# A split-precision GRU graph kernel: the products of gates r and z with the aggregate, reordered into high part first and low part last

## What is computed

```
A = (adj != 0).astype(x.dtype)
h = x
for l in range(weight.shape[0]):            # 5 layers
    m = jnp.einsum('bnd,de->bne', h, weight[l])
    agg = jnp.einsum('bij,bid->bjd', A, m)
    h = _gru_cell(agg, h, w_ih, w_hh, b_ih, b_hh)

def _gru_cell(m, h, w_ih, w_hh, b_ih, b_hh):
    gi = m @ w_ih.T + b_ih
    gh = h @ w_hh.T + b_hh
    i_r, i_z, i_n = jnp.split(gi, 3, axis=-1)
    h_r, h_z, h_n = jnp.split(gh, 3, axis=-1)
    r = sigmoid(i_r + h_r)
    z = sigmoid(i_z + h_z)
    n = tanh(i_n + r * h_n)
    return (1.0 - z) * n + z * h
```

## Time and profile before

| | before |
|---|---|
| median of 3 runs | 631.34 us |
| the profiled execution's own time | 631.32 us |
| its span, first to last instruction | 629.2 us |
| mean granted TensorE clock | 0.994 |
| PE busy | 611.5 us, 97% of the span, 2933 matmuls |
| DVE busy | 509.3 us, 81% |
| ACT busy | 411.7 us, 65% |
| POOL busy | 366.6 us, 58% |

### The profile page before, as it was taken

One profiled execution on the slowest core, in us unless ns is written; L12 is line 12 of the kernel. 1 busy time (PEld: TensorE's weight loads), 2 busy tenths in 40 slices (PEclk: granted clock), 3 DMA queues, 4 the chain that ended last, 5 costly groups with the idle time before them and its releaser, 6 DMA issues.

```text
span 629.2 us, 10158 instructions
## 1 busy us (share of the span) xinstructions
PE 611.5 (97%) x2933; PEld 499.0 (79%) x2933; DVE 509.3 (81%) x1163; ACT 411.7 (65%) x777; POOL 366.6 (58%) x299
## 2 busy tenths in 40 slices
PE   7899999999999999999999999999999999999993
PEld 5677888888888888888888888888888888888772
DVE  5987878897878889788897979889797887967677
ACT  4866776758567685766758576675866758564551
POOL 0644645658566565765658576565756657564343
PEclk9999999999999999999999999999999999999997
DMA  7532312220231313022230322223023230000001
GB/s 269 210 101 68 101 67 84 84 101 17 83 100 67 100 47 121 32 83 86 80 100 17 103 81 67 100 83 100 17 83 100 67 100 0 17 0 1 18 0 51
DMA packets 37999, 47.28 MB, mean 75 GB/s; under 512 B 1760, under 2 KB 19680, under 8 KB 37984
## 3 DMA queue, kind: packets, MB, share of 16 engines
q1 hardware_dynamic: 37712, 46.97, 22.7%
q10 hardware_dynamic: 272, 0.13, 0.1%
HBM read 42.90 MB, written 4.19 MB: 75 GB/s over the span
## 4 chain that ended last, share of the span: by engine, by line
PE 92%; DVE 4%; DMA 1%; issue 1%; SPq 1%; ACT 1%; POOL 0%; POOLq 0%; DVEq 0%
PE ps_tok L1244 12%; PE ps_tok L1251 12%; PE ps_r L1109 6%; PE ps_r L1111 6%; PE ps_r L1110 6%; PE ps_z L1111 6%; PE ps_z L1109 6%; PE ps_z L1110 6%; PE ps_tok L1104 5%; PE ps_b L1109 3%; PE ps_b L1111 3%; PE ps_b L1110 3%; PE ps_b L1104 3%; PE ps_in L1110 3%; PE ps_hn L1111 3%; PE ps_in L1109 3%
## 5 line engine op out<-in xcount | busy, mean ns | idle before, releaser
L557 POOL TENSOR_TENSOR h_lo<-h,h_hi 128x512 fp32r<-128x512 f32 x64 | 83.0, 1297 | 113.8 <-ACT h_hi L587 113.8
L567 POOL TENSOR_TENSOR z_h<-z_gate,h 128x512 f32<-128x512 f32 x80 | 109.9, 1374 | 42.8 <-ACT z_gate L764 42.8
L587 ACT ACTIVATE tok_hi<-ps_tok 128x512 fp32r<-128x512 f32 x63 | 37.7, 599 | 102.2 <-PE ps_tok L1104 102.2
L1088 DVE SCALAR_TENSOR_TENSOR r_hn<-ps_hn,gru_bias,r_gate 128x512 f32<-128x512 f32 x80 | 59.9, 749 | 42.6 <-ACT r_gate L754 41.6
L1244 PE MATMUL ps_tok<-edges,tok_hi 128*128 (+1 forms) x320 | 88.0, 397 | 0.7 <-ACT tok_hi L587 0.7
L1251 PE MATMUL ps_tok<-edges,tok_lo 128*128 (+1 forms) x320 | 87.7, 396 | 0.0
L687 ACT ACTIVATE ps_in<-ps_in,gru_bias 128x512 f32<-128x512 f32 x80 | 52.8, 660 | 52.5 <-DVE ps_in L978 52.4
L507 POOL TENSOR_TENSOR adjt_lo<-adjt_in,adjt_hi 128x512 fp32r<-128x512 f32 x56 | 71.7, 1302 | 4.3 <-ACT adjt_hi L587 4.3
L1244 PEld LDWEIGHTS ps_tok<-edges,tok_hi 128*128 128x128 f32 x320 | 59.8, 188 | 15.5 <-ACT tok_hi L587 0.9
L1251 PEld LDWEIGHTS ps_tok<-edges,tok_lo 128*128 128x128 f32 x320 | 59.9, 188 | 14.8 <-DVE tok_lo L790 0.3
L790 DVE TENSOR_TENSOR tok_lo<-ps_tok,tok_hi 128x512 fp32r<-128x512 f32 x63 | 43.6, 692 | 30.0 <-ACT tok_hi L587 28.4
(11 more groups left out here) (144 smaller groups left out, 1582.6 us busy)
## 6 DMA issues: line engine op xcount, KB each, us to landing
adjt_in<-in_adj_t_dram SPq DMA_DIRECT2D x14, 1024.0 KB, 5.3
adj_in<-in_adj_dram SPq DMA_DIRECT2D x14, 1024.0 KB, 5.5
x_in<-in_x_dram SPq DMA_DIRECT2D x16, 256.0 KB, 2.8
xt_in<-in_x_t_dram SPq DMA_DIRECT2D x15, 256.0 KB, 2.6
out_dram<-y_out SPq DMA_DIRECT2D x15, 256.0 KB, 2.3
adjt_in<-in_adj_t_dram SPq DMA_DIRECT2D x4, 256.0 KB, 4.0
adj_in<-in_adj_dram SPq DMA_DIRECT2D x4, 256.0 KB, 6.8
second_adjt<-in_adj_t_dram SPq DMA_DIRECT2D x1, 1024.0 KB, 6.9
```

The source lines that it names most:

```text
L557: nc.gpsimd.tensor_tensor(h_lo[new][:], h[new][:], raw(h_hi[new][:]), ALU.subtract).then_inc(s_h_lo, 1)
L567: nc.gpsimd.tensor_tensor(z_h[:], z_gate[:], h[own][:], ALU.mult).then_inc(s_zh, 1)
L587: return nc.scalar.activation(dst, src, ACT.Copy)
L1088: nc.vector.scalar_tensor_tensor(out=r_hn[:], in0=ps_hn[:], scalar=bhh_cols[:, 2:3], in1=r_gate[:], op0=ALU.add, op1=ALU.mult).then_inc(s_ ...
```

## The change

The three products of each gate keep their operands and their banks, but their order changes. Before: r high by high, r with the aggregate's low part, r with the weights' low part; then the same for z. After: r's two products with `agg_hi`, z's two products with `agg_hi`, then r's product with `agg_lo`, then z's with `agg_lo`. `s_r_sum` is raised by the fifth of the six matmuls instead of the third, `s_z_sum` by the sixth as before. The wait for `s_agg_lo` ahead of the gate products becomes a wait for `s_agg_hi`, and a wait for `s_agg_lo` stands between the fourth and the fifth product. Where the slot has a turn, a wait for `s_agg_lo` stays ahead of the turn.

```diff
@@ -1269,8 +1269,6 @@
                     if w.prepares() and slot == 4 and not w.ramps():
                         first_state()
-                    if unit:
-                        pe.wait_ge(s_agg_lo, w.units(slot + 1))
                     if w.next_turned(slot):
 
                         v, s = w.next_turned(slot)
@@ -1278,6 +1276,8 @@
                         pe.wait_ge(s_h, v.until_made(s))
                         if w.leads():
                             pe.wait_ge(s_own, w.prepared(2, 2))
+                        if unit and not w.leads():
+                            pe.wait_ge(s_agg_lo, w.units(slot + 1))
                         for c in range(C):
                             last = turn(turned_bank(w)[:, c * P:(c + 1) * P], h[t][:, c * P:(c + 1) * P])
                         last.then_inc(s_tok, 1)
@@ -1294,8 +1294,14 @@
                     if unit:
                         wi_hi, wi_lo = wc_hi[:, layer, :], wc_lo[:, layer, :]
-                        gate(ps_r, 0, agg_hi, agg_lo, wi_hi, wi_lo, False, True).then_inc(s_r_sum, 1)
-                        gate(ps_z, 1, agg_hi, agg_lo, wi_hi, wi_lo, False, True).then_inc(s_z_sum, 1)
+                        pe.wait_ge(s_agg_hi, w.units(slot + 1))
+                        for dst, g in ((ps_r, 0), (ps_z, 1)):
+                            gs = slice(g * D, (g + 1) * D)
+                            nc.tensor.matmul(dst[:], wi_hi[:, gs], agg_hi[:], start=False, stop=False)
+                            nc.tensor.matmul(dst[:], wi_lo[:, gs], agg_hi[:], start=False, stop=False)
+                        pe.wait_ge(s_agg_lo, w.units(slot + 1))
+                        nc.tensor.matmul(ps_r[:], wi_hi[:, 0:D], agg_lo[:], start=False, stop=True).then_inc(s_r_sum, 1)
+                        nc.tensor.matmul(ps_z[:], wi_hi[:, D:2 * D], agg_lo[:], start=False, stop=True).then_inc(s_z_sum, 1)
                         if w.first > 0 or slot > 0:
                             pe.wait_ge(s_h, w.units(slot))
                         gate(ps_in, 2, agg_hi, agg_lo, wi_hi, wi_lo, True, True).then_inc(s_in_sum, 1)
```

## The result

| | before | after |
|---|---|---|
| median | 631.24 us (630.56 to 631.48, 4 runs) | 635.69 us (635.26 to 636.33, 4 runs) |
| the profiled execution's own time | 631.32 us | 635.26 us |
| its span | 629.2 us | 633.2 us |
| mean granted TensorE clock | 0.994 | 0.993 |

The ratio is 1.0073, with a 95% interval of 1.0056 to 1.0091: 4.45 us slower. 3.4 us more and 634.7 us were forecast. One execution among all runs of this document, in the kernel with the new order everywhere but in slot 4, took 873.86 us at a mean granted clock of 0.656; it is not compared with the others.

What follows compares the result with a forecast made beforehand. PE, busy 97% of the 629.2 us span, was taken to bound the kernel. The terms 0 + 2.2 + 0.3 + 0.5 + 0.46 = 3.4 us gave 634.7 us, range 632.3 to 636.6.

Steps and rivals of the forecast that it cites:

- unit 0 to unit 2: Unit 0's stand of 0.39 us goes, lost again at unit 2's first state product: 0, bounds -0.39 and +0.07.
- slot 0, 13 windows: First state product waits for POOL's later `h_lo`: 0.17 us per window, 2.2 us in all, bounds 0.5 and 3.5.
- turn of slot 3, 13 windows: Turn's load, waiting for `agg_lo`, 0.18 late with 0.16 hidden: 0.02 per window, 0.3 us, bounds 0 and 1.0.
- turns of units 74, 76, 78: Turns standing on the `h` of the unit before pay its delay in full: 0.15, 0.18, 0.15, sum 0.5 us.
- the end: The last unit's later r starts a chain through last turn, norm and store that nothing covers: 0.46 us.
- the load follows a released wait by 0.06: 297.41, 0.27 late: At slot 0: `h_lo` ends at 297.35, so the waiting load starts at 297.41 instead of 297.14.
- the last `r_gate` to the end is as long as before: Expected sign in the changed kernel's profile: the stretch from the last `r_gate` to the end keeps its length.
- Rival A: The load's 0.23 lead hides the late load; each slot 0 window costs 0.04: 633.1 or 632.7 us; chance 0.14.
- Rival B: Only the end pays, the delay not reaching POOL or margins larger: 0.6 to 1.0 us, 632.1 us; 0.11 with Case D.
- Rival C: Not slower: four `agg_hi` products in a row bring gate distances to 0.226, returning 3.4 us: 631.3 us; chance 0.08.
- Case D: The change does nothing, since 63 of 80 waits stay where they are; chance 0.11 together with Rival B.

Runs made afterwards that it cites:

- r third: The changed kernel with its waits kept, but r's three products first again, so r is complete with the third matmul: 630.44 us, ratio 0.9995 to the kernel before.
- r fourth: Against r third, z's first product with `agg_hi` moved ahead of r's with `agg_lo`, so r is complete with the fourth matmul: 631.05 us, ratio 1.0004.
- the split kernel: Against the changed kernel, slot 0's first `ps_hn` product waits for `h_hi` alone, the wait for `h_lo` moves to the second: 632.40 us, ratio 1.0026.
- the slot 4 kernel: The change in slot 4 of windows 2 to 14 alone, 13 units of 80, the rest as before: 633.94 us, ratio 1.0046 to the kernel before.
- r sixth: Against the changed kernel, r's product with `agg_lo` put behind z's, so r is complete with the sixth matmul: 642.98 us, ratio 1.0195 to the kernel before.

## Why the prediction was right, point by point

The predicted 634.7 us lies 1.0 below the 635.69 measured, inside the range. **Direction, place and mechanism** came as forecast: slower, because r's sum is later and the first state product of slot 0 waits 13 times for POOL's `h_lo`. r third and r fourth show that it is r's place that matters, the split kernel that it is that wait, and the slot 4 kernel that 13 units are enough for it.

| term | forecast us | measured us, from starts of matmuls |
|---|---|---|
| unit 0 to unit 2 | 0 | -0.40 + 0.28 + 0.20 = +0.1 |
| slot 0, 13 windows | 2.2 | 2.9 |
| turn of slot 3, 13 windows | 0.3 | 0.5 (0.03 each, 0.09 in the first) |
| turns of units 74, 76, 78 | 0.5 | 0.10 + 0.11 + 0.11 = 0.3 |
| the end | 0.46 | 0.71 |
| sum | 3.4 | 4.5; 4.45 between the medians |

The terms cover nearly all: from unit 0's start on, the starts of matmuls and the end give 4.7 us. The spans of the two profiles differ by 4.0 only, since in the profiled execution of the kernel after the part ahead of unit 0, which the change does not touch, was 0.6 shorter; the spans of two other executions of it are 634.3 and 633.9.

**The mis-sized term is slot 0.** The step that was off is "the load follows a released wait by 0.06: 297.41, 0.27 late". In the twelve windows of the loop the load followed POOL's `h_lo` by 0.13, in the change, r fourth, r sixth and the slot 4 kernel alike. That and 0.49 in place of 0.46 for `h_lo` make the load 0.37 late instead of 0.27. What was hidden, 0.12, lies near the 0.10 taken from rows 6. So the slots 0 lost 2.9 us where 2.2 were forecast, 0.7 of the 1.0 us that was missing.

**Where the 0.13 comes from** is in the traces. It is not POOL: in the thirteenth window, unit 71 behind the loop, POOL makes the same `h_lo`, and the load follows it by 0.05:

```profile
560.97 1.30 POOL L562 TENSOR_TENSOR h_lo<-h,h_hi 128x512 fp32r<-128x512 f32 x1 [0.43 <-ACT h_hi L587]
...
562.32 0.19 PEld L1109 LDWEIGHTS ps_hn<-h_hi,whh_hi 128*128 128x128 f32 x1 [0.31 <-POOL h_lo L562]
```

The first product of a slot 0 has two waits, for `h_lo` and for `r_hn`. The semaphore records show which instruction holds which. In unit 71, as in the unit 2 of rows 5, the load itself holds the wait for `h_lo`. In the loop the load holds the wait for `r_hn`, and that for `h_lo` is held by an instruction of the sequencer ahead of it (PEldq), 12 times:

```profile
L1206 PEldq FUSED_REGOPS  x12: 42/42/42, 109.9 to 524.6; - x12
```

That instruction starts 0.04 behind `h_lo`, and the load 0.09 behind it. This is also why those loads are named "issue", as were the three turns of the earlier trace rows: the view names only what the load itself waited for. The same step is seen in two other places. In the split kernel, in the loop, the second product's load holds the wait for `h_lo` and follows it by 0.05. At the turns of units 74, 76 and 78 the kernel before holds the wait for `h` ahead of the load, which follows `h` by 0.12; in the change the two waits have changed places, the load holds the one for `h`, and follows by 0.05. So rows 5 were a place of the other kind than the slots 0 of the loop.

**Units 0 to 2** were right in the sum, and half right in the way. 0.40 was gained. Of it, 0.27 was lost behind unit 1, where the first aggregate product of unit 2 stood for `tok_hi`, which the prediction had in ACT's queue but not as something that PE stands for. 0.14 was lost at unit 2's first state product, which stands on `h_lo` as forecast, and some 0.06 around its turn.

**The turn of slot 3** was right with its reason: ACT was late in slot 2 (`r_gate` 0.15 later there, 0.46 to 0.48 in the other slots), and a turn hides 0.16 of a late load.

**The turns of units 74, 76 and 78** were right in the delay of `h` (0.17 + 0.18 + 0.16 us later), but the load now follows `h` by 0.05 instead of 0.12, so 0.3 us was paid and not 0.5. Here the moved wait gave something back, which no step had.

**The end** was right with 0.46 for the chain: PE stands 3.66 us instead of 3.20 ahead of the last turn. The other 0.25 comes from the clock of the four transposes, which no step had (below). So the sign "the last `r_gate` to the end is as long as before" held for the chain and not for these. It is luck that this 0.25 and the 0.2 not paid at the late turns nearly cancel in the sum.

**Rival A**, that the lead hides the late load, is false as a whole and true in part. The Trainium skill, "TensorE: Matmul & The Clock Gate", section on the array's architecture, says that a matmul can begin before its weight load completes. r fourth agrees: its load leads its matmul by 0.12 only, while the load's own record is 0.19 long. But not all of the 0.23 of lead is to be had. Counted from the last aggregate matmul, a load of `ps_hn` that is 0.11 late cost 0.01 (r fourth), 0.22 cost 0.10 (new order everywhere but in slot 4), 0.26 cost 0.14 (unit 71 of the change), 0.35 cost 0.23 (the loop of the change) and 0.58 cost 0.46 (r sixth): all but about 0.12 is paid.

**Rival B** (only the end pays) falls with the 13 stands. **Rival C** (the new order streams better) falls with the timeline of a slot 1, beside the earlier trace rows:

```profile
312.23 0.40 PE L1300 MATMUL ps_r<-agg_hi,wc_hi 128*128 128x512 f32 x1
...
314.33 1.10 PE L1244 MATMUL ps_tok<-edges,tok_hi 128*128 x4
```

Nine products take 2.10 us, as before. Case D fell with the rest.

## What to carry to other kernels

Reordering products moves the time at which each bank is complete, so hold the move against the margin of every wait of PE that follows from that bank: here one matmul (0.23 us) of delay cost at most some tenths in all, two cost 4.45 us, three cost 12.2. Where two roads lead a delay to one instruction, undoing one of them brings back less than its share, so a split into halves need not add up. And take the latency behind a wait from a place where the same instruction holds it: here it was 0.05 us where the load held the wait, and 0.12 to 0.13 where an instruction ahead of it did.

## What was not expected of the hardware

**The last transposes differ by 0.4 us between kernels that end alike.** PE stands for 3.2 us or more ahead of them. Stretches around them, with PE busy (x), PEld, DVE, ACT and POOL, then the granted clock. Before:

```profile
620.60:621.80 1.20, 0.82 (x4) 0.43 (x4) 1.04 (x9) 0.00 (x0) 0.28 (x1) 0.68 0.00 0
```

After:

```profile
624.40:625.90 1.50, 1.07 (x4) 0.67 (x4) 1.09 (x9) 0.00 (x0) 0.57 (x1) 0.56 0.00 0
```

The split kernel:

```profile
620.90:622.40 1.50, 0.66 (x4) 0.42 (x4) 1.43 (x9) 0.00 (x0) 0.22 (x1) 0.92 0.00 0
```

With a mean granted clock of 0.92 the four take 0.66 us, with 0.68 0.82, with 0.56, near the lower level of 1.2 GHz, 1.07; r fourth and r sixth have 1.12, r third 0.66. (The stretches reach past the transposes, so the clock is that of the stretch.) The clock falls after PE has stood, but where the fall lies against the transposes differs from profile to profile, and the length of the stand does not set it: the split kernel stood about as long as the change. What sets where the fall lies is not shown. Such a quarter of a microsecond in a single profile is not evidence for an edit.

**A row of waits can be free.** The loads for `ps_hn` of the twelve slots 0 in the loop stood 1.9 us in r fourth and cost less than 0.1; in the change they stood 4.7 us and cost 2.8.
